# Zero products in the image attention, linear scores ahead in odd steps, and finer waits, in a fused float32 model kernel on one core

## The reference

```
q2 = elu(q2) + 1.0001 ; k2 = elu(k2) + 1.0001
num = q2 @ cumsum(k2^T v2) ; den = q2 . cumsum(k2) + 1e-4 ; so = num / den
x2 = x + (ao @ proj + norm(so @ ssm_out)) @ out_w + out_b
x3 = x2 + gelu(norm(x2) @ w1 + b1) @ w2 + b2
```

## Time and profile before

| what | us |
|---|---|
| median of 3 runs | 806.16 (806.01 to 810.58) |
| profiled execution | 807.84 |
| its span, first to last instruction | 806.1 |
| TensorE busy in the span | 746.5 (93%) |
| VectorE, ScalarE, GpSimd busy | 306.4, 240.8, 171.9 |
| mean granted clock of TensorE | 0.955 |

### The profile page before, as it was taken

One profiled execution on the slowest core, in us unless ns is written; L12 is line 12 of the kernel. 1 busy time (PEld: TensorE's weight loads), 2 busy tenths in 40 slices (PEclk: granted clock), 3 DMA queues, 4 the chain that ended last, 5 costly groups with the idle time before them and its releaser, 6 DMA issues.

```text
span 806.1 us, 16998 instructions
## 1 busy us (share of the span) xinstructions
PE 746.5 (93%) x6882; PEld 537.8 (67%) x6882; DVE 306.4 (38%) x785; ACT 240.8 (30%) x516; POOL 171.9 (21%) x220
## 2 busy tenths in 40 slices
PE   7998788998999989898899999889999999999987
PEld 7357455666666747667557666488888888888455
DVE  2165456556527636634241661211111111111243
ACT  0203234455545464543322300112222222221101
POOL 5452122263103112210010035100000010000470
PEclk9897699999999999979899999899999999999999
DMA  9500000540000000000000033179999999993131
GB/s 324 205 1 2 1 11 11 196 160 2 2 2 11 2 1 12 2 1 2 11 1 1 10 120 151 60 288 354 352 368 345 366 344 366 347 373 109 49 97 42
DMA packets 33662, 102.75 MB, mean 127 GB/s; under 512 B 5033, under 2 KB 19390, under 8 KB 28224
## 3 DMA queue, kind: packets, MB, share of 16 engines
q1 hardware_dynamic: 23328, 69.09, 23.3%
q10 hardware_dynamic: 5760, 23.60, 8.5%
q0 software_dynamic: 4512, 9.19, 3.4%
HBM read 90.45 MB, written 9.83 MB: 124 GB/s over the span
## 4 chain that ended last, share of the span: by engine, by line
PE 79%; DVE 10%; issue 4%; ACT 3%; another core or an unknown queue 3%; POOL 0%; DVEq 0%; ACTq 0%; POOLq 0%
PE PS L1492 11%; PE PS L2058 9%; PE PS L2170 8%; PE PS L2174 5%; PE PS L2071 4%; PE PS L1689 3%; PE PS L2186 3%; PE PS L2142 2%; PE PS L1498 2%; PE PS L1758 2%; PE PS L1777 2%; PE PS L1742 1%; PE PS L2191 1%; PE PS L1700 1%
## 5 line engine op out<-in xcount | busy, mean ns | idle before, releaser
L2058 PE MATMUL PS<-X,w_sgu 64*128 64x512 f32 x432 | 104.2, 626 | 7.3 <-DVE gu L1332 7.2
L1453 DVE TENSOR_TENSOR rh<-rsg,PS 128x768 f32<-128x768 f32 x32 | 30.5, 955 | 160.5 <-ACT rsg L914 160.5
L2058 PEld LDWEIGHTS PS<-X,w_sgu 64*128 64x128 f32 x432 | 43.1, 196 | 59.5 <-issue 44.8
L2170 PE MATMUL PS<-xt,w_rgu 128*128 128x128 f32 x576 | 70.3, 277 | 1.3 <-ACT xt L893 1.3
L2170 PEld LDWEIGHTS PS<-xt,w_rgu 128*128 128x128 f32 x576 | 67.5, 192 | 3.7 <-issue 1.9
L622 POOL DMA_DIRECT2D y_slots<-ys x32 | 17.4, 545 | 225.3 <-ACT ys L900 225.3
L914 ACT ACTIVATE rsg<-PS 128x768 f32<-128x768 f32 x32 | 26.0, 811 | 127.0 <-PE PS L2174 96.2
L2071 PEld LDWEIGHTS PS<-w_sdn,gu 128*128 128x128 f32 x288 | 46.6, 190 | 6.9 <-issue 3.8
L542 POOL TENSOR_TENSOR rs<-ve,minus_half 128x3 f32<-128x3 f32 x12 | 10.4, 863 | 190.5 <-DVE ve L1182 190.5
L1492 PE MATMUL PS<-w_rdn,rh 128*128 128x192 f32 x288 | 50.9, 327 | 0.0
L2071 PE MATMUL PS<-w_sdn,gu 128*128 128x192 f32 x288 | 49.1, 329 | 1.8 <-DVE gu L1332 1.8
(11 more groups left out here) (356 smaller groups left out, 1318.4 us busy)
## 6 DMA issues: line engine op xcount, KB each, us to landing
w_rgu<-in_wgu SPq DMA_DIRECT2D x24, 1152.0 KB, 9.0
w_pgu<-in_wgu SPq DMA_DIRECT2D x16, 1152.0 KB, 8.3
w_rdn<-in_wd ACTq DMA_DIRECT2D x24, 576.0 KB, 5.3
w_pdn<-in_wd ACTq DMA_DIRECT2D x16, 576.0 KB, 6.6
x_slots<-zeros SPq DMA_DIRECT2D x1, 3072.0 KB, 19.5
xs<-x_slots SPq DMA_DIRECT2D x32, 96.0 KB, 3.9
y_slots<-ys POOLq DMA_DIRECT2D x32, 96.0 KB, 6.6
w_sgu<-in_shared_gu SPq DMA_DIRECT2D x2, 1152.0 KB
```

The source lines that it names most:

```text
L1453: dve.tensor_tensor(rh[:, j, :], rsg[:, j, :], PS[:, 2:4, :].rearrange("p a b -> p (a b)")[:, 0:FF], ALU.mult).then_inc(S["r_h"], 1)
L2058: mm = pe.matmul(PS[:, 2 * y + n % 2, :], w_sgu[rows_y, e, c, cols_m], x[rows_y, :], start=(c == 0), stop=(c == 2), skip_group_check=True)
L2170: pe.matmul(dst(y, m), w[:, y, 128 * m:128 * m + 128], xt[:, j, y, :], start=(m % 4 == 0), stop=False, skip_group_check=True)
```

## The change

1. Normalisation of patch tile i - 1 directly behind the statistics of tile i; the position table's sums ahead of the last one.
2. `tok_up` starts with the first half of its input (`ready`), here and in the second layer.
3. The values of the image attention go to banks 6 and 7, behind the last text sum; `pb2` is read ahead of the first maximum; the transposes of tile 0 no longer wait for the copies `tv`.
4. `keep_going(n)`: n products of zeros into bank 0; 3 and 2 of them behind the transposes of tiles 2 and 3, 2 behind the last product with the values, 1 behind the last turn.
5. The last projection does each half to its end before the other.
6. Ahead of the pair loop: image tile 1 is turned in bank 7 alone, the values of sequence 1 go to banks 2 and 6 and wait for `k_out` instead of `p_xn`, and the loop starts with two reads of values instead of four; the waits that go are set later, in the fillers of step (0, 0).
7. In odd steps the linear scores come behind `turn_weights(u - 1, 0)`, and the linear values behind `turn_weights(u - 1, 1)`.
8. At the end the last `gate_times_up` comes ahead of `add_routed(2)`.

The diff, cut to its core:

```diff
-                act.activation(tv[:, 4 * k:4 * k + 4, :, 0:DH], PS[:, 4 + k, 0:VB0].rearrange("p (w k e) -> p w k e", w=4, e=DH), ACT.Copy
+                act.activation(tv[:, 4 * k:4 * k + 4, :, 0:DH], PS[:, 6 + k, 0:VB0].rearrange("p (w k e) -> p w k e", w=4, e=DH), ACT.Copy
...
-            images_out(1, PS[:, 2, 0:128], PS[:, 7, 0:128])
+            images_out(1, PS[:, 7, 0:128], PS[:, 7, 128:256])
...
+            def patch_norm(i):
+                dve.wait_ge(S["a_rs"], i + 1)
+                dve.tensor_scalar(zA[:, i, :], PS[:, i, 0:D], mv[:, i, 0:1], rs[:, i:i + 1], ALU.subtract, ALU.mult
+                                  ).then_inc(S["a_z"], 1)
+
             for i in range(IT):
                 dve.wait_ge(S["patch_mm"], i + 1)
                 statistics(PS[:, i, 0:D], i, 1e-5, st[:, 0, :], mv, ve).then_inc(S["a_ve"], 1)
-            for i in range(IT):
-                dve.wait_ge(S["a_rs"], i + 1)
-                dve.tensor_scalar(zA[:, i, :], PS[:, i, 0:D], mv[:, i, 0:1], rs[:, i:i + 1], ALU.subtract, ALU.mult
-                                  ).then_inc(S["a_z"], 1)
+                if i >= 1:
+                    patch_norm(i - 1)
             dve.wait_ge(ld_tok, 2 * 16)
             for c in range(2):
                 ins = dve.tensor_scalar(pe_tab[:, c, :], pe_tab[:, c, :], col("tok_ln_b", c), None, ALU.add)
+            patch_norm(IT - 1)
...
+            dve.wait_ge(S["a_pb"], 2)
+            dve.tensor_tensor(pb2[:, :], PS[:, 4:6, VB0], cols[:, COLS["tok_proj_b"]:COLS["tok_proj_b"] + 2], ALU.add
+                              ).then_inc(S["a_pb"], 1)
             less_maximum(0)
             dve.wait_ge(S["h_txt"], B)
             norm_statistics(in_h, text_tiles, "p_ve1")
             dve.wait_ge(S["a_sub"], 1)
             less_maximum(1)
-            dve.wait_ge(S["a_pb"], 2)
-            dve.wait_ge(S["a_v"], 2)
-            dve.tensor_tensor(pb2[:, :], PS[:, 4:6, VB0], cols[:, COLS["tok_proj_b"]:COLS["tok_proj_b"] + 2], ALU.add
-                              ).then_inc(S["a_pb"], 1)
...
-            values_out(0, 1, (2, 7))
+            values_out(0, 1, (2, 6))
...
-            gate_times_up(n + 8, n + 10)
+            gate_times_up(n + 8, n + 11)
             dve.wait_ge(S["e_acc"], 4 * EARLY + 4)
             add_routed(2)
-            gate_times_up(n + 11, n + 11)
...
-            def in_pairs(w, k, x, a, b, done):
-
+            def in_pairs(w, k, x, a, b, done, ready=None):
+
+                if ready is not None:
+                    pe.wait_ge(S[ready], 1)
                 pe.matmul(PS[:, a, :], w[:, k, 0, :], x[:, 0, :], start=True, stop=False, skip_group_check=True)
+                if ready is not None:
+                    pe.wait_ge(S[ready], 2)
                 pe.matmul(PS[:, b, :], w[:, k, 1, :], x[:, 1, :], start=True, stop=False, skip_group_check=True)
                 pe.matmul(PS[:, a, :], w[DR:128, k, 2, :], x[DR:128, 1, :], start=False, stop=True, skip_group_check=True
                           ).then_inc(S[done], 1)
                 pe.matmul(PS[:, b, :], w[0:DR, k, 2, :], x[0:DR, 0, :], start=False, stop=True, skip_group_check=True
                           ).then_inc(S[done], 1)
 
-            def tok_up(src, base, bank0):
+            def tok_up(src, base, bank0, ready):
                 for k in range(3):
                     if k == 2:
                         pe.wait_ge(S["a_h"], base + 2)
-                    in_pairs(w_tff1, k, src, bank0 + 2 * k % 4, bank0 + 2 * k % 4 + 1, "a_ff1")
+                    in_pairs(w_tff1, k, src, bank0 + 2 * k % 4, bank0 + 2 * k % 4 + 1, "a_ff1", ready if k == 0 else None)
 
             pe.wait_ge(ld_tok, 2 * 16)
-            pe.wait_ge(S["a_x"], 2)
-            tok_up(xT, 0, 0)
+            tok_up(xT, 0, 0, "a_x")
...
+            def keep_going(n):
+
+                for _ in range(n):
+                    pe.matmul(PS[:, 0, 0:D], ones_sq[:, :], zeros[:, :], start=True, stop=True)
...
+            pe.wait_ge(S["t_rd"], B)
...
-                        pe.matmul(PS[64 * half:64 * half + 64, 4 + k, 96 * (w % 4):96 * (w % 4) + 96], y1T[:, 0, IMG * w:IMG * w + IMG],
+                        pe.matmul(PS[64 * half:64 * half + 64, 6 + k, 96 * (w % 4):96 * (w % 4) + 96], y1T[:, 0, IMG * w:IMG * w + IMG],
...
-            pe.wait_ge(S["a_v"], 2)
...
                 if i + 2 < IT:
                     img_scores(i + 2)
+                else:
+                    pe.wait_ge(S["a_sub"], IT)
+                    keep_going(IT + 1 - i)
                 if i >= 1:
                     img_turn_outputs(i - 1)
                     pe.wait_ge(S["a_at"], i)
                 else:
-                    pe.wait_ge(S["t_rd"], B)
+                    pe.wait_ge(S["a_v"], 2)
...
+            keep_going(2)
             img_turn_outputs(IT - 1)
+            keep_going(1)
             pe.wait_ge(S["a_at"], IT)
-            for c in range(2):
+            for c, rows_c in enumerate(REST):
                 pe.matmul(PS[:, 2 + c, :], w_tproj[:, c, :], aTA[:, c, :], start=True, stop=False, skip_group_check=True)
-            for c, rows_c in enumerate(REST):
...
-            pe.wait_ge(S["a_x1"], 2)
-            tok_up(y1T, FM, 2)
+            tok_up(y1T, FM, 2, "a_x1")
...
-                        pe.wait_ge(S["k_out"], 1)
+                        pe.wait_ge(S["p_xn"], 4)
...
+                        pe.wait_ge(S["phi_e"], 2)
+                        pe.wait_ge(S["phi_r"], 2)
                         image_down(2)
...
+                def linear():
+
                     pe.wait_ge(S["ab_read"], TURN["l", q, j])
                     if j in (0, 4):
                         pe.wait_ge(S["phi"], 2 * q + 1 + j // 4)
                         pe.wait_ge(S["phi_k"], 2 * q + 1 + j // 4)
                     linear_scores(q, j)
+
+                behind_heads = j % 2 == 1 and q < PAIRS
+                if q < PAIRS:
+                    masked()
+                if turning:
+                    turn_weights(u - 1, 0)
+                if behind_heads:
+                    linear()
+                elif turning:
+                    linear_values(u - 1)
+                if turning:
+                    turn_weights(u - 1, 1)
+                if behind_heads:
+                    linear_values(u - 1)
+                first_filler(q, j)
+                if q < PAIRS and not behind_heads:
+                    linear()
                 second_filler(q, j)
                 if turning:
                     soft_values(u - 1)
@@ -2032,13 +2057,11 @@
             pe.wait_ge(shifted, 32)
             project(0, 0, (5, 6), (2,))
             project(0, 1, (3, 4), (2,))
-            turn_images(1, PS[:, 2, 0:128], PS[:, 7, 0:128])
+            turn_images(1, PS[:, 7, 0:128], PS[:, 7, 128:256])
             project_values(0, 0, (0, 1))
-            pe.wait_ge(S["p_xn"], 4)
-            project_values(0, 1, (2, 7))
-            pe.wait_ge(S["v_out"], 4)
-            pe.wait_ge(S["phi_e"], 2)
-            pe.wait_ge(S["phi_r"], 2)
```

14 lines of the change are left out of this document (4 added, 10 removed).

## The result

The changed kernel takes **845.23 us** (median of 4 runs, 842.38 to 849.02) against 807.43 us for the kernel before in the same comparison: ratio **1.0465**, 95% interval 1.0402 to 1.0529, so 4.6% slower. The forecast was 826.4 with a range up to 838: the direction holds, the size does not.

What follows compares the result with a forecast made beforehand. TensorE, with 79% of the chain, was taken to bound the kernel. Parts 1 to 6 gave -3.4 us, part 7 +20.4 and the loop's clock +3.2: +20.2 on 806.16, so 826.4 us, range 813 to 838.

Steps and rivals of the forecast that it cites:

- Clock in the loop: Pair loop: new pauses in 12 steps bring two more half-clock stretches of TensorE, +3.2 us, bounds 0 and +10.
- rival B: Pair loop: each of 12 odd steps also brings a half-clock stretch, 842 us in all; chance 0.08.
- Part 7: Odd steps of the pair loop: linear scores first wait for VectorE's masked copy, +20.4 us, bounds 13 and 22.
- Part 3: Image attention: eight zero products cost +2.3 us on the path, and an earlier clock rise gives -1.5.
- Parts 1, 2 and 4: Patches and first projection, image values, last projection: TensorE starts earlier or waits less, -1.0, -1.6 and -0.8 us.
- Part 5: Ahead of the pair loop: two waits go, but most of up to 2.8 us becomes a later wait, -0.5 us.
- Part 6: Kernel's end: the last gate product moves ahead of a routed addition and TensorE's 0.28 us wait goes, -0.3 us.
- C: Pair loop: VectorE and ScalarE set its end, TensorE recovers odd-step losses in even steps; -3.9 or -6.5 us, chance 0.07.
- E: Pair loop: second waits stay hidden, pairs 0 and 3 lose nothing, clock falls no oftener; 810 us, chance 0.05.
- D: Image attention: the clock stays full from 68.6 us on, giving back 8 us more; 818 us, chance 0.10.
- what was to show the forecast wrong: Copy before heads' read, even steps shrinking by odd ones' growth, or attention clock dip gone and worth over 8 us.

Runs made afterwards that it cites:

- e1: The changed kernel with the old order of the odd steps, all else kept: 800.42 us, ratio 0.9944 to the kernel before.
- e3b: The changed kernel with zero products filling the pauses ahead of the linear scores of odd steps: 808.22 us, ratio 1.0119 to the kernel before.
- e6: e1 without the eight products of zeros in the last two image tiles: 809.3 us, ratio 1.0009 to the kernel before.
- e16: e5 without the eight products of zeros in the image tiles, on the chip of e15: 807.11 us, ratio 1.0008 to the kernel before.
- e15: The same kernel as e5, run on another chip: 801.56 us, ratio 0.9924 to the kernel before.
- e12: e1 with 40 zero products in the pause of step (0, 0): 801.76 us, ratio 0.9922 to the kernel before.
- e14: e1 with 12 zero products in the pause of (0, 0) and 5 in that of (0, 1): 799.47 us, ratio 0.9902 to the kernel before.
- e2: The kernel before with only the order of the odd steps changed: 857.09 us, ratio 1.0674.
- e9: The kernel before, order unchanged, with linear values of odd steps made to wait for VectorE's masked copy: 836.97 us, ratio 1.0481.
- e5: The changed kernel with the old order of odd steps and the loop start as before: 786.08 us, ratio 0.9834 to the kernel before.

## Why the prediction was too low

**The step that failed is "Clock in the loop": +3.2, bounds 0 and +10.** It was to be some 18 us: the ten steps cost 38.9 us in the changed kernel and 20.7 with the same waits filled. Over the whole loop it is 20.7 us of longer busy time against e1. The mechanism was seen, and put into rival B at 0.08 (842 us; measured 845). I counted two new stretches for twelve new pauses because of slices 7 to 11 of before, which show none. But before had only pauses of up to 1.3 us in these steps; ten of the twelve are 1.9 to 2.9 us now (two are 0.8), and I had no row of such a pause within dense work to say that it would leave the clock alone. The Trainium skill, "TensorE: Matmul & The Clock Gate", section "A second HAM failure mode: psum-queue depth-cycling", says of another kernel, in bf16, that frequent short idles between groups of matmuls make the clock swing, and that the throughput suffers by the "re-throttle/re-warm cost paid between bursts". The traces agree: 3.90 us instead of 2.21 for the products behind a pause. Rival B, which I had put beside that rule, says 842. Its count nearly holds too: every odd step but (0, 5) has a stretch at half clock, and the seven from (1, 1) to (3, 1) have one of 3.4 us each. That it comes so near to 845 is in part luck, since it had the front at -3.4 and no part 5 in its clock.

**Part 7's price in waits held.** 18.6 us forecast for ten steps, 20.7 measured in e3b. The single steps are near as well: (1, 1) 1.6 against 1.79, (1, 3) 2.3 against 2.29, (1, 5) 2.4 against 2.65; and (2, j) the same. The second waits came as named: state products behind ScalarE, turns of z 1.28 instead of 1.05 us. In (0, 1), +1.5 against 2.04 in waits, but 8.06 with the clock.

**Part 3, zeros: +2.3 and -1.5, net +0.8; wrong in sign.** They are worth 5 to 7 us by the ratios (e6, e16), of which the traces show the start of the loop, 1.8 us earlier with them (e15) than without (e16), and 4.3 between e1 and e6. The clock rises at 81 to 83 us in most traces with them (after, e1, e15; in e12 and e14 it doesn't fall there at all) and at 95 to 98 in all five without (before, e2, e6, e9, e16). For that I allowed 1.5 us of gain, and the term is too small. What the eight products cost by themselves no run separates from it.

**Parts 1, 2 and 4: -3.4 forecast, between -1.4 and -3.9 measured.** e16 has them without zeros and early start, and its loop starts at 125.5 against 129.33. But in its trace the image attention is at half clock for 17 us, in the one before for 27, so part of the 3.9 is clock. In e6 it is so for 31 us; its loop starts at 124.9, and without the 3.0 of part 5 that leaves 1.4. The direction held, the size is right only to within that.

**Part 5: -0.5.** Without the clock it is near zero, as argued (3.0 us earlier, 2.9 back in the wait for GpSimd's va). With the clock it costs 6 us in the traces (step (0, 2) starts at 151.0 in e1, at 144.8 and 144.9 in e5 and e15), since a half-clock stretch comes with its pauses. By the ratios (0.9944 against 0.9924 in e15) a cost isn't shown. The same omission as in the failed step.

**Part 6: -0.3.** The wait of the earlier trace rows is gone; the last products are one run without idle time before or in them:

```profile
829.67 8.07 PE L2094 MATMUL PS<-w_sdn,gu 128*128 128x192 f32 x48
```

What that is worth in the time no run tells; nothing speaks against 0.3.

The other rivals: C (faster) and E are out, as part 7 alone costs 6.7% (e2). D holds in part: the attention's clock does rise earlier, but the loop took more than that back. Of what was to show the forecast wrong, nothing came: the copy still stands behind the heads' read, no even step shrank by what odd ones grew, and the dip in the attention is still there. The failure lay in something that this list didn't have.

Together: the waits (18.6 forecast, 20.7 measured) were right and parts 1, 2, 4 about right, the clock was mis-sized by some 15 us in the ten steps, more than the better front could make good.

## What to carry to other kernels

A new wait of 2 us in front of dense products on TensorE has two prices: itself, and the slower clock behind it. Here the second was as large as the first (20.7 and 19.3 us in the loop). Before moving a consumer ahead, compare its releaser's place in the other engine's queue with that of the consumer which it displaces: the heads' read came first, the copy second, so the swap could only wait. And where a pause can't be removed, products of zeros that just fit it (0.22 us each here) buy back the clock; what outlasts the pause is paid in full. And take the worth of an edit from the steps of the traces that it can reach: here code that no edit touched differed by 15 us between two chips.

## What was not expected of the hardware

A wait of 2.18 us, with no other change, turned twelve products of 2.21 us into 3.90 (e9). A pause of 2.88 us was followed by 13.7 us at half clock, although TensorE had no idle time in them, and one of 2.18 us in (1, 3) by 3.4. That it isn't the pause's length alone shows in e12, where 13.6 us at half clock follow a pause of 1.26 us in the same step (0, 1); why this step's falls last so long was not tried. The same kernel in two profiled executions had different stretches (e5 and e15 agree up to (3, 3), and step (3, 4) differs by 3.1 us), and its ratio on two chips was 0.983 and 0.992: of such a kernel, differences under 1% need both on one chip.
